# Attention stage of a gated cross-attention block: row statistics in one group a slot, the bias in the batch product, attended values copied by ScalarE and multiplied on GpSimd

## The reference

```python
h   = layernorm(x)                                   # encoder_hc
Sim = (h @ w1)[:, :, None] + (ctx @ w2)[:, None, :] + einsum(h * w3, ctx) + b_sim
A   = softmax(Sim, axis=2);  hq_hat = A @ ctx
Batt = softmax(max(Sim, axis=2), axis=1);  hc_bar = Batt @ h      # one row a batch
hcq = concat([h, hq_hat, h * hq_hat, h * hc_bar]) @ W_qv + b_qv
x1  = x + tanh(g_xattn) * hcq
y   = layernorm(x1)                                  # goes to the feed-forward network
out = x1 + tanh(g_ffn) * ffn(y)
```

## Time and profile before

| | us |
|---|---|
| median of three runs | 452.32 |
| the profiled execution | 453.42 |
| its span, first to last instruction | 451.6 |
| attention stage, from 0 to about | 190 |
| TensorE busy in the span | 419.8 (93%) |
| VectorE busy | 357.7 (79%) |
| ScalarE busy | 295.0 (65%) |
| GpSimd busy | 114.5 (25%) |

### The profile page before, as it was taken

How to read it: one execution, slowest core, us unless ns; L and a number is a source line. 1 busy time by engine, 2 the same in 40 slices (tenths; PEclk the granted TensorE clock), 3 DMA queues, 4 the chain that set the end, 5 groups by cost and what they waited for, 6 DMA issues and landing times.

```text
span 451.6 us, 7009 instructions
## 1 busy us (share of the span) xinstructions
PE 419.8 (93%) x2466; PEld 289.2 (64%) x2466; DVE 357.7 (79%) x681; ACT 295.0 (65%) x412; POOL 114.5 (25%) x128
## 2 busy tenths in 40 slices
PE   3887999999789599999999999999999999999997
PEld 2776899889678599644444444444444444788886
DVE  4768698987897667784444699999998889897884
ACT  2568658667847244484334699998387779987760
POOL 1243644756459733100000013343000000000000
PEclk9969999999999979999999999999999999999999
DMA  6970000200200020200000000000000000344442
GB/s 210 292 239 15 1 1 1 96 0 2 92 2 1 1 93 1 93 1 1 0 0 0 0 0 0 0 0 1 0 0 0 0 1 2 120 137 141 139 140 71
DMA packets 21086, 21.41 MB, mean 47 GB/s; under 512 B 981, under 2 KB 20804, under 8 KB 21060
## 3 DMA queue, kind: packets, MB, share of 16 engines
q1 hardware_dynamic: 21040, 21.08, 14.7%
q10 hardware_dynamic: 20, 0.00, 0.0%
HBM read 12.69 MB, written 8.39 MB: 47 GB/s over the span
## 4 chain that ended last, share of the span: by engine, by line
PE 41%; DVE 26%; issue 20%; ACT 8%; SPq 2%; DMA 2%; POOL 1%; POOLq 0%; DVEq 0%; ACTq 0%
PE ps L842 12%; PE ps L807 9%; PE ps L812 5%; DVE cols L1547 4%; PE ps L634 2%; DVE hid L1563 2%; PE ps L638 2%; DMA xa<-in_x 2%; ACT hid L1098 2%; DVE st L1278 2%; DVE xa L1274 2%; PE ps L588 1%; DVE st L1191 1%; DVE sc L1229 1%; ACT ag L1103 1%
## 5 line engine op out<-in xcount | busy, mean ns | idle before, releaser
L807 PE MATMUL ps<-xh,wuh 128*128 128x512 f16 x192 | 72.8, 379 | 0.8 <-DVE gq L1586 0.8
L807 PE MATMUL ps<-xh,wul 128*128 128x512 f16 x192 | 72.8, 379 | 0.0
L812 PE MATMUL ps<-xl,wuh 128*128 128x512 f16 x192 | 57.1, 379 | 0.0
L1526 DVE TENSOR_REDUCE cols<-hid x10 | 22.9, 2286 | 24.3 <-ACT hid L1075 24.3
L842 PE MATMUL ps<-wdl,oh 128*128 128x256 f16 x168 | 37.4, 273 | 0.0
L842 PE MATMUL ps<-wdh,oh 128*128 128x256 f16 x168 | 37.4, 273 | 0.0
L1075 ACT ACTIVATE hid<-ps 128x2048 f32 x10 | 18.8, 1875 | 27.5 <-PE ps L812 27.5
L807 PE MATMUL ps<-xh,wgh 128*128 128x512 f16 x96 | 36.4, 379 | 0.0
L807 PE MATMUL ps<-xh,wgl 128*128 128x512 f16 x96 | 36.4, 379 | 0.0
L513 POOL PARTITION_ALL_REDUCE cols<-cols x4 | 1.5, 378 | 134.9 <-DVE cols L1486 134.9
L807 PEld LDWEIGHTS ps<-xh,wuh 128*128 (+1 forms) x192 | 18.8, 98 | 24.0 <-issue 1.8
(11 more groups left out here) (254 smaller groups left out, 1100.0 us busy)
## 6 DMA issues: line engine op xcount, KB each, us to landing
x_scratch<-xa SPq DMA_DIRECT2D x4, 1024.0 KB, 4.4
xo<-x_scratch SPq DMA_DIRECT2D x16, 256.0 KB, 2.7
out_dram<-xo SPq DMA_DIRECT2D x15, 256.0 KB, 2.2
xa<-in_x SPq DMA_DIRECT2D x3, 1024.0 KB, 11.0
xa<-in_x SPq DMA_DIRECT2D x4, 256.0 KB, 5.7
wv<-in_L_xattn_W_qv SPq DMA_DIRECT2D x1, 1024.0 KB, 8.5
wr<-in_L_ffn_w_gate SPq DMA_DIRECT2D x1, 768.0 KB, 7.1
wr<-in_L_ffn_w_up SPq DMA_DIRECT2D x1, 768.0 KB, 9.2
```

The source lines that it names most:

```text
L807: pe.matmul(ps[hf][:, q, :], w_[:, d, ds(k * P, P)], xh[:, d, n], start=d == 0 and w_ is wh, stop=False)
L812: mm = pe.matmul(ps[hf][:, q, :], wh[:, d, ds(k * P, P)], xl[:, d, n], start=False, stop=d == KD - 1)
L1526: dve.tensor_reduce(gmx[:, ds(k * 2 + hf, 1)], unit(hid, k, hf), AX.X, ALU.max, apply_absolute_value=True).then_inc(gm_done, 1)
```

## The change

- The statistics of x (task m+3) and those of the new x (task m-7) are taken in one group a slot (`both_stats`), four statistics and one set of aggregations, ahead of `scored`. The small operations behind them (adding epsilon, the negative mean, the product of mean and deviation) go from VectorE to GpSimd (`both_std`).
- `norm_x` on VectorE stays for the first four tasks only; ScalarE does it from task 4 (before: from 8).
- b_qv is split in two parts and added to the context's product inside TensorE (two more matmuls of two rows a batch, L572 in the new file; the weights of the softmax sum to one). `bias_x` on GpSimd goes.
- `attended` goes from VectorE to ScalarE, as a copy from PSUM to prT, and GpSimd multiplies it by h (`product`).
- The weights `we` of the first three batches are made by ScalarE (`batch_scaled`) and GpSimd (`batch_weights`); VectorE still makes those of the last (`last_weights`).
- The product of the first context goes to another PSUM bank, and is done behind the other steps of its slot; `batch_cols` and `summary` of batches 1 and 2 stand earlier in their slot; `project` is cut in two parts in every slot; and in slot 18 VectorE splits the weights before the summary.

```diff
-        NF = 2 * NP
+        NF = NP
+        YG = LAG + 3
+            def both_std(g):
+                r, q = g % 4, slice(0 if g < N else 2, 2 if g < YG else 4)
+                pool.wait_ge(mv_done, g + 1)
...
+                pool.tensor_scalar(vp[:, r, q], mv[:, r, q, 1], LN_EPS, 1.0, ALU.add, ALU.mult)
+                pool.tensor_scalar(nmean[:, r, q], mv[:, r, q, 0], -1.0, 1.0, ALU.mult, ALU.mult).then_inc(own_done, 1)
+                pool.wait_ge(own_done, 2 * (g - NP) + 1)
+                pool.tensor_tensor(rstd[:, r, q], vp[:, r, q], mhalf[:, q], ALU.pow).then_inc(own_done, 1)
+                pool.wait_ge(own_done, 2 * (g - NP) + 2)
+                pool.tensor_tensor(nmr[:, r, q], nmean[:, r, q], rstd[:, r, q], ALU.mult).then_inc(std_rdy, 1)
-            def bias_x(n):
-                pool.tensor_tensor(x_, x_, txb[:].unsqueeze(1).broadcast_to([P, 2, D]), ALU.add).then_inc(xb_rdy, 1)
+            def product(n):
+                pool.wait_ge(hqT_rdy, n + 1)
+                pool.wait_ge(hT_rdy, n + 1)
+                pool.tensor_tensor(prT[:, par, :, q], prT[:, par, :, q], hT[:, par, :, q], ALU.mult).then_inc(pr_rdy, 1)
+            def batch_weights(b):
+                pool.wait_ge(ws_rdy, b + 1)
+                pool.tensor_tensor(w_, w_, wv[:, 0:KD, :], ALU.add).then_inc(we_rdy, 1)
...
             def context_project(b):
+                seen = y_bank if b == 0 else m_bank
+                for o_, j in ((seen[0:JM, 0:D], slice(0, JM)), (seen[0:JS, D:2 * D], slice(JM, JM + JS))):
+                    for d in range(KD):
+                        pe.matmul(o_, cxT[:, d, j], wv[:, KD + d, :], start=d == 0, stop=False)
+                    mm = pe.matmul(o_, minus[0:2, 0:j.stop - j.start], bhl[0:2, :], start=False, stop=True)
...
-                ge(pe, pr_rdy, n)
+                ge(pe, hqT_rdy, n)
...
+            def attended(n):                       # on ScalarE
+                act.wait_ge(hq_ps, n + 1)
+                act.activation(prT[:, par, :, s * PT:(s + 1) * PT], hq_bank.rearrange("p (d n) -> p d n", d=KD),
+                               ACT.Copy).then_inc(hqT_rdy, 1)
+            def batch_scaled(b):                   # on ScalarE
+                act.wait_ge(hc_rdy, b + 1)
+                for d in range(KD):
+                    a_ = act.activation(we[:, b % 2, d, :], wv[:, 3 * KD + d, :], ACT.Copy, scale=c_hc[:, d:d + 1])
+                a_.then_inc(ws_rdy, 1)
...
+            def both_stats(g):                     # on VectorE
+                if g < N:
+                    for t in range(2):
+                        i_ = dve.bn_stats(st[:, t, :], xa[:, 2 * g + t, :])
+                if g >= YG:
+                    dve.wait_ge(x1_rdy, g - YG + 1)
+                    for t in range(2):
+                        i_ = dve.bn_stats(st[:, 2 + t, :], xa[:, 2 * (g - YG) + t, :])
+                i_.then_inc(bn_done, 1)
+                dve.wait_ge(bn_done, g + 1)
+                dve.wait_ge(std_rdy, g - 3)
+                for t in range(0 if g < N else 2, 2 if g < YG else 4):
+                    i_ = dve.bn_aggr(mv[:, g % 4, t, :], st[:, t, :])
+                i_.then_inc(mv_done, 1)
...
             for m in range(N + LAG):               # the slot loop of ScalarE
+                if s == 3 and 1 < b < B:
+                    batch_scaled(b - 1)
...
+                if 3 <= m <= N + 2:
+                    attended(m - 3)
                 if 1 <= m <= N:
                     normed(m - 1)
+                if s == 3 and b == 1:
+                    batch_scaled(b - 1)
```

More of the change, by code:

```diff
@@ L173, in build @@
     cbi = place(a, "cbi", [P, 2, J], F32)
[L174 removed]
+    row = place(a, "row", [1, 3], F32)
+    brow = place(a, "brow", [2, D], F32)
+    bhl = place(a, "bhl", [2, D], F32R)
+    minus = place(a, "minus", [2, P], F32R)
     w2b = place(a, "w2b", [P, KD, P], F32)
@@ L480, in _ @@
                 b, s = m // NP, m % NP
[L481 to L486, removed]
+                if 4 <= m <= N + 3:
+                    product(m - 4)
+                if s == 3 and 1 <= b < B:
+                    batch_weights(b - 1)
                 if s == 1 and 1 <= b < B or m == N:
@@ L752, in _ @@
                     score(m - 1)
-                if LAG <= m and not late:
-                    project(m - LAG, b - 1 if s == 1 and b < B else None)
-                if LAG <= m and late:
-                    project_first(b - 1)
-                if s == 2 and b < B:
+                if m == L + LAG:
+                    project_last()
+                elif LAG <= m:
+                    project_first(m - LAG)
+                    if s == 1 and b < B:
+                        batch_max(b - 1)
+                    if not late:
+                        project_rest(m - LAG)
+                if s == 3 and 1 < b < B:
+                    batch_cols(b - 1)
+                if s == 2 and 2 <= b < B:
                     context_project(b)
@@ L1431, in _ @@
                     weights_low(m - 3)
+                if m == N + 2:
+                    summary(b - 1)
+                    last_weights()
                 if m == 0:
                     norm_x(3)
-                if 3 <= m and m + 1 < NF:
-                    norm_x(m + 1)
-                if NF <= m + 1 < N:
-                    row_shift(m + 1)
                 if s == 0 and 1 <= b < B:
@@ L1441, in _ @@
                     batch_shift(b - 1)
+                if s == 3 and 2 <= b < B:
+                    summary(b - 1)
                 if LAG < m:
@@ L1448, in _ @@
                     residual(m - LAG)
+                if 1 <= m and (m + 3 < N or LAG <= m) and not (LAG <= m and late):
+                    if s == 1 and m + 3 < N:
+                        dve.wait_ge(xr_in[b], 16)
+                    both_stats(m + 3)
                 if 1 <= m < N:
```

276 lines of the change are left out of this document (119 added, 157 removed).

## The result

The changed kernel takes **458.25 us** (median of four runs, 457.76 to 459.48) against 452.94 us of the kernel before, run beside it: ratio 1.0119, 95% interval 1.0084 to 1.0154. It is slower by 1.2%; 448.8 us was forecast, and 458.25 lies outside the range. The profiled execution has a span of 457.7 us against 451.6, so the traces have 6.1 us to explain (it took 459.48 us, the longest of the four, so 6.1 is a little more than the 5.3 between the medians).

A forecast was written before the change was run, and what follows sets the result against it. TensorE was taken to bound slots 8 to 22, VectorE near behind, a ScalarE-VectorE round before slot 8. Terms -11.6 - 3.4 + 0.5 + 2.5 + 0 + 3.0 + 2.0 + 3.2 + 0.3 = -3.5 gave 448.8 us; 8-in-10 range 442.5 to 456.

The forecast's parts named there:

- start: Task 0's scores 2.05 us later behind task 4's statistics, set against TensorE's 2.15 us wait: +2.5 us, bounds 0 and +5.
- slots 4 to 6: VectorE is relieved and ScalarE loaded, 16.5 us before and after: 0, bounds -3 and +3.
- slot 7: Batch 0's `we` through ScalarE and GpSimd delays `project_rest(0)`: +3.0 us, bounds +1 and +4.
- low clock behind slot 7: TensorE's 4 us idle in slot 7 brings the low clock: +2.0 us, bounds 0 and 3.4.
- matmuls: Two extra matmuls of two rows a batch on TensorE: +0.5 us, bounds 0 and 1.2.
- new waits: Slots 8 to 18: the round through `norm_y`, residual, scores and division binds in some slots: +3.2 us, bounds 0 and +10.
- last y: Last row of y passes two more small GpSimd operations and less of VectorE: +0.3 us, bounds 0 and 0.6.
- The end of slot 18: Split ahead of summary: task 15's attention doesn't wait, and the low clock after that wait goes, 3.4 us.
- VectorE's relief: TensorE's waits for VectorE go: 6.6 us between 57 and 153 us plus 4.96 before 157.98, 11.6 us.
- Rival A: VectorE was everything: start free, slot 7 without low clock, half the new waits: 442.7 us; chance 0.18.
- Rival B: Slots 8 to 17: ScalarE's round through `norm_y` becomes the bound, 1.48 us a slot: 456.0 us; chance 0.18.
- Rival C: Start at its upper bound and another microsecond in slots 4 to 6: 452.3 us; chance 0.16.

The follow-up runs named there:

- e7: Kernel before with one edit: in slot 18 VectorE makes task 14's attended product and task 15's low weights ahead of the summary and `we`; 451.82 us, 0.9983.
- e4: Changed kernel with GpSimd's up-weight scaling behind task 11's statistics and ScalarE's down-weight conversion behind its `norm_y`, at the end of slot 18; 455.70 us, 1.0073.
- e13: Changed kernel with only the start (task 0's scores, batch 0's context product) in the order of the kernel before; 455.30 us, 1.0065.
- e5: Changed kernel with GpSimd's slot 6 reordered: low part of batch 1's context and batch 0's summary additions ahead of task 2's product and the statistics; 456.94 us, 1.0101.
- e14: Changed kernel with the orders of e4, e5 and e11 (old start), every operation on the engine the change gave it; 450.92 us, 0.9960.
- e11: e8 with the start in the order of the kernel before (task 0's scores and batch 0's context product earlier); 446.47 us, 0.9873.
- e15: e11 with TensorE's context product of batch 1 moved in slot 6 as in e9; 445.76 us, 0.9870.
- e9: e8 with TensorE's context product of batch 1 ahead of turning task 4's weights in slot 6, not behind task 3's attention; 449.95 us, 0.9943.
- e8: Changed kernel with work of slots 3 to 7 shared out as before, plus the edits of e5 and e4; 451.29 us, 0.9975.

## Why the prediction was wrong

Against the table of the two traces, by the prediction's own steps:

| step | forecast | measured |
|---|---|---|
| start | +2.5 | +3.05 |
| slots 4 to 6 | 0 | +0.93 |
| slot 7 | +3.0 | +4.07 |
| low clock behind slot 7 | +2.0 | +1.7 |
| slots 8 to 18: VectorE's waits -11.6, matmuls +0.5, new waits +3.2 | -7.9 | -7.1 |
| low clock of slot 18 -3.4, last y +0.3 | -3.1 | +3.2 |
| feed-forward | 0 | +0.3 |
| sum | -3.5 | +6.1 |

**The step that failed** is "The end of slot 18": "`attend` of task 15 doesn't wait ... The low clock that followed the wait goes too". The first half is true. But the 4.96 us had been cover: the residual, the statistics and `norm_y` of task 11 ran in them, and I asked only whether `last_weights` would be late next, not y. The trace of the kernel before had the number: y was ready 1.7 us before TensorE turned it, so no more than 1.7 us of the wait could come back, where I booked all 4.96, and 3.4 of low clock. `we` and ScalarE's conversion stood ahead of that round before, too; in the changed list GpSimd's 2.77 us of scaling falls into it as well. With the low clock it makes 6.3 of the 9.6 us of error, by the row of the table on slot 18. e7 shows it without the rest of the change (8.4 expected by that step, some 0.8 measured), e4 shows the new wait's price in the changed kernel (2.1 us of time, 3.5 in the trace).

**Start, slots 4 to 6, slot 7.** A loss was forecast for the start and for slot 7, and none for slots 4 to 6; each came out 0.5 to 1.1 us too small. For the start I set TensorE's vanished wait of 2.15 us against the context product moved behind `turn_a`; the product was in fact in no wait any more (it now takes TensorE 3.5 us, from 23.41), and e13 prices the two moves at 3.7 us in the trace. For slots 4 to 6 the sum of ScalarE's list was right (16.5 us forecast, 16.47 busy), but not the whole: the stretch took 17.46, with 0.96 of idle time in which ScalarE waited for turned h, behind the product of batch 1 on TensorE. For slot 7 I counted from "the same 53.56" and called GpSimd "Hidden". Its low part of the context ended 6.7 us late and held the attention of task 4, and by it ScalarE's copy of the attended values, for 0.76 us (e5 gives that back). I had followed GpSimd only where it makes `we`, and TensorE's turning of the context, which no part of the sum has, not at all. The low clock of slot 7 came as forecast, and the first scores at 19.52 us, near the 19.8.

**VectorE's relief** was right: the waits between 57 and 153 us that named it shrank from 6.6 to 2.2 us, and the gain over slots 8 to 18 is 0.8 us short of the forecast. The waits from slot 8 to the attention of task 15 sum to 3.8 us (forecast about 3), but name VectorE (2.2) more than ScalarE (0.95) and GpSimd (0.63). Rival A's premise (start and slot 7 free) is refuted by both. Rival B gave nearly the right time, 456.0, by the wrong mechanism: `norm_y` doesn't pace slots 8 to 17, in which TensorE waits for it 0.95 us in all and ScalarE is idle for 22.4 of 90.2 us (70.45 to 160.62). Rival C named the start as the place, rightly, and stopped at 452.3.

The Trainium skill ("SBUF — State Buffer", Who interferes with whom) has a VectorE instruction with two SBUF inputs, as the `we` instruction is, and a GpSimd instruction that reads SBUF exclude each other. The trace fits again: 2.10 us for the pair beside L440, and L440 itself 1.73 where its twin took 1.48. TensorE didn't wait for `we` in slot 18; what the 2.10 us delayed was the residual behind it.

## What to carry to other kernels

A wait that goes is worth no more than the distance to the next thing that is late (here 1.7 us of 4.96): before booking it, walk the other chains that ran in its shadow, to the moment at which each is needed, with the new orders in them. While this pipeline filled, busy shares said little: GpSimd was busy for 5.50 of 15.50 us in slots 3 to 5, and yet TensorE waited 3.40 us for it in slot 7. A move that relieves the busiest engine of the steady state can be right from the first full slot on and wrong before it, and the two can be given different sharings. Both the orders and the sharing counted: the orders alone took the change from 1.2% slower to 0.4% faster (e14), the old sharing in slots 3 to 7 to 1.3% faster (e11).

## Of the hardware

Executions of one kernel differ, in most cases with their mean granted clock. Those of e15 at 1.000 took 444.4 and 445.0 us, the one at 0.989 448.35; those of e9 448.4 at 1.000 and 451.0 to 451.2 at 0.989. That is 2.6 to 3.9 us between executions of one program, more than several of the effects sought here. It isn't the only thing that moves them: in the times of e4 and e8 no such order is seen (e8: 450.4 us at 0.988, 451.6 at 0.996).

A wait whose releaser the profile leaves open ("issue") can be for any engine, and a releaser near in time is no proof. Of the two in slot 7, the one of 0.90 us went with GpSimd's work (e5). The one of 0.56 us kept its length in the changed kernel, e5 and e8, while the distance from GpSimd's last addition to its end was 0.66, 1.2 and 3.25 us; it ended each time 0.1 us behind ScalarE's copy of the turned context.
